# Two graph layers on one core: a new order of small steps at both ends of a graph, and another preparation of the first graph

## The reference, cut to what matters

```python
# layer 0
e0    = leaky(einsum('bid,bjd->bij', x * a0[:, 0], x))      # leaky: v if v >= 0 else 0.2 v
alpha = sigmoid(where(adj == 1, e0, -inf))
x     = layernorm(x + einsum('bij,bjd->bid', alpha, x) + bias)
# layer 1
Hh    = x @ W
s, d  = Hh @ a[:256], Hh @ a[256:]
e     = where(adj != 0, exp(-leaky(s[:, None] + d[None, :])), 0)
x     = layernorm(x + elu((e @ Hh) / rowsum(e)))
```

## Time and profile before

| | before |
|---|---|
| three runs, us | 1290.22, 1290.91, 1291.21 (median 1290.91) |
| profiled execution, us | 1292.38 |
| its span, us | 1290.6 |
| busy, share of the span | PE 94%, weight loads 88%, POOL 81%, DVE 77%, ACT 77% |
| chain that ended last | DVE 34%, POOL 31%, "issue" 22%, PE 6%, ACT 4% |

### The profile page before, as it was taken

How to read it: one execution, slowest core, us unless ns; L and a number is a source line. 1 busy time by engine, 2 the same in 40 slices (tenths; PEclk the granted TensorE clock), 3 DMA queues, 4 the chain that set the end, 5 groups by cost and what they waited for, 6 DMA issues and landing times.

```text
span 1290.6 us, 29789 instructions
## 1 busy us (share of the span) xinstructions
PE 1212.5 (94%) x8898; PEld 1135.5 (88%) x8898; DVE 997.1 (77%) x2499; ACT 988.9 (77%) x2290; POOL 1045.2 (81%) x1052
## 2 busy tenths in 40 slices
PE   5899999999999999999999999999999999999985
PEld 4789899898998989899898988989898898988875
DVE  4678778787877878778787877878778787878855
ACT  4677878778787887878788787887878788787763
POOL 2779797887988889797887988889797887978864
PEclk9999999999999999999999999999999999999988
DMA  9467390854828366381854828366381854818301
GB/s 192 90 118 137 58 178 27 154 106 86 166 40 150 78 131 129 57 164 39 154 106 78 174 37 148 83 129 126 62 162 42 154 106 70 182 34 147 56 9 36
DMA packets 223634, 135.31 MB, mean 105 GB/s; under 512 B 141168, under 2 KB 207088, under 8 KB 223600
## 3 DMA queue, kind: packets, MB, share of 16 engines
q1 hardware_dynamic: 188528, 84.57, 28.0%
q0 software_dynamic: 35072, 50.34, 26.0%
HBM read 101.32 MB, written 16.78 MB: 92 GB/s over the span
## 4 chain that ended last, share of the span: by engine, by line
DVE 34%; POOL 31%; issue 22%; PE 6%; ACT 4%; DVEq 1%; POOLq 1%; DMA 0%; ACTq 0%
POOL coef_lo L394 9%; POOL coef_lo L402 8%; DVE coef L1010 6%; DVE coef L940 5%; POOL rstd L434 3%; DVE stats L1052 3%; DVE reluP L1047 3%; DVE xt_bank L1044 3%; DVE stats L958 2%; DVE coef L931 2%; DVE resid L953 2%; DVE gT_lo L884 2%; POOL var_eps L431 2%; POOL coef_lo L408 2%; POOL h_lo L385 2%
## 5 line engine op out<-in xcount | busy, mean ns | idle before, releaser
L394 POOL TENSOR_TENSOR coef_lo<-coef,coef_hi 128x1024 fp32r<-128x1024 f32 x128 | 307.0, 2405 | 57.4 <-DVE x L970 32.1
L1253 PE MATMUL acc_bank<-h_hi,coef_hi 128*128 128x256 f32 x1024 | 302.5, 295 | 16.6 <-ACT reluP L702 13.9
L402 POOL TENSOR_TENSOR coef_lo<-coef,coef_hi 128x1024 fp32r<-128x1024 f32 (+1 forms) x128 | 294.5, 2308 | 11.5 <-ACT coef_hi L636 11.1
L1253 PE MATMUL acc_bank<-H_hi,coef_hi 128*128 128x258 f32 x1024 | 296.0, 289 | 7.4 <-ACT reluP L702 5.4
L1254 PE MATMUL acc_bank<-H_lo,coef_hi 128*128 128x258 f32 x1024 | 290.6, 284 | 0.0
L1255 PE MATMUL acc_bank<-H_hi,coef_lo 128*128 128x258 f32 x1024 | 290.2, 283 | 0.0
L1255 PE MATMUL acc_bank<-h_hi,coef_lo 128*128 128x256 f32 x1024 | 285.9, 279 | 0.0
L1254 PE MATMUL acc_bank<-h_lo,coef_hi 128*128 128x256 f32 x1024 | 285.8, 279 | 0.0
L1253 PEld LDWEIGHTS acc_bank<-h_hi,coef_hi 128*128 128x128 f32 x1024 | 193.7, 189 | 26.7 <-issue 22.4
L1010 DVE SCALAR_TENSOR_TENSOR coef<-tr_bank,E_col,codeT 128x256 f32<-128x256 f32 (+1 forms) x384 | 193.0, 565 | 24.2 <-POOL coef_lo L402 21.7
L1253 PEld LDWEIGHTS acc_bank<-H_hi,coef_hi 128*128 128x128 f32 x1024 | 194.3, 190 | 11.2 <-issue 8.3
(11 more groups left out here) (91 smaller groups left out, 2814.7 us busy)
## 6 DMA issues: line engine op xcount, KB each, us to landing
code_nat<-in_adj POOLq DMA_DIRECT2D x128, 256.0 KB, 4.8
x_raw<-in_x SPq DMA_DIRECT2D x16, 1024.0 KB, 6.5
xb<-bias_bc SPq DMA_DIRECT2D x16, 1024.0 KB, 8.7
xb<-in_x POOLq DMA_DIRECT2D x16, 1024.0 KB, 12.2
out<-x SPq DMA_DIRECT2D x128, 128.0 KB, 2.0
codeT<-code_nat SPq DMA_TRANSPOSE x128, 3.5
W_ext<-in_L_gnn_W SPq DMA_DIRECT2D x1, 256.0 KB, 3.9
x1T<-in_L_gnn_a SPq DMA_DIRECT2D x1, 256.0 KB, 5.1
```

The source lines that it names most:

```text
L394: nc.gpsimd.tensor_tensor(coef_lo[:, t % 4, :, :], blocks(coef[:, t % 4, :]), f32(coef_hi[:, t % 4, :, :]), ALU.subtract).then_inc(S.lo0, 1)
L402: nc.gpsimd.tensor_tensor(coef_lo[:, t % 4, j0:NT, :], blocks(coef[:, t % 4, j0 * P:N]), f32(coef_hi[:, t % 4, j0:NT, :]), ALU.subtract).t ...
L1253: nc.tensor.matmul(dst, lhs_hi, rhs_hi, start=first, stop=False)
```

## The change

It has two parts. At the borders, in every graph: DVE takes `norm0(7)` ahead of the mask of columns 3 and 4; it takes `residual1(6)` ahead of `mask0_rest(2)`, `row_inverse(7)` between the two, and `residual1(7)` ahead of the whole mask of tile 3; ACT takes `keep_H(6)` and `keep_x1T(7)` ahead of `high1_begin`, the four `high_x` later and spread out, and `high0(b+1, 2)` behind `elu_parts(7)`, `high0(b+1, 3)` behind `tanh_row(b+1, 6)`.

```diff
@@ DVE, graph @@
                     if t == 8:
                         low_H(F, b, 5)
-                        mask1_tiles(b, 0, 4, 3, EDGE)
                         keep_watch(b, prev)
...
+                mask1_tiles(b, 0, 4, 3, EDGE)
                 if nxt:
                     leaky_scores(b + 1, 3)
                 low_H(F, b, 6)
...
                 for t in range(NT):
-                    if t >= 3:
+                    if 3 <= t < 7:
                         row_inverse(F, b, t, prev)
-                    if t >= 4 and nxt:
+                    if 4 <= t < 7 and nxt:
                         mask0_below(b + 1, t - 4, True)
+                    if 4 <= t < 6 and nxt:
                         mask0_rest(b + 1, t - 4)
                     residual1(F, b, t, prev)
                     stats1(F, b, t)
                     moments1(F, b, t)
+                    if t == 6:
+                        row_inverse(F, b, 7, prev)
+                        if nxt:
+                            mask0_rest(b + 1, 2)
+                    if t == 7 and nxt:
+                        mask0_below(b + 1, 3, True)
+                        mask0_rest(b + 1, 3)
@@ ACT, graph @@
                     scale_scores(b + 1, 3)
-                high1_begin(b)
-                if nxt:
-                    high_x(F, b + 1, 0)
                 keep_H(F, b, 6, prev, False)
                 keep_x1T(F, b, 7, prev)
-                if nxt:
-                    high_x(F, b + 1, 1)
+                high1_begin(b)
+                if nxt:
                     scale_scores(b + 1, 4)
...
                 high1(F, b, 1)
                 if nxt:
-                    high_x(F, b + 1, 2)
+                    high_x(F, b + 1, 0)
                     scale_scores(b + 1, 7)
                 high1(F, b, 2)
+                if nxt:
+                    high_x(F, b + 1, 1)
                 high1(F, b, 3)
                 for t in range(NT + 1):
                     if nxt and t == 0:
                         scale_scores(b + 1, 8)
-                        high_x(F, b + 1, 3)
+                        high_x(F, b + 1, 2)
...
                     if t == 1:
                         high1(F, b, 4)
                         if nxt:
+                            high_x(F, b + 1, 3)
                             scale_row(b + 1, 3)
...
-                    if t + 3 >= NT and nxt:
-                        high0(F, b + 1, t + 3 - NT, True)
+                    if nxt and t in (5, 6):
+                        high0(F, b + 1, t - 5, True)
+                    if nxt and t == NT:
+                        high0(F, b + 1, 2, True)
                     if nxt and 3 <= t:
                         tanh_row(b + 1, t - 2)
+                    if nxt and t == NT:
+                        high0(F, b + 1, 3, True)
```

```diff
@@ SP @@
-            load_x(F, 0)
+            for q in range(2):
+                tiles = slice(NT - 2 * q - 2, NT - 2 * q)
+                sp.dma_start(x_raw[:, tiles, :], x_v[0, :, tiles, :]).then_inc(x_part[q], 16)
+            tiles = slice(0, NT // 2)
+            sp.dma_start(x_raw[:, tiles, :], x_v[0, :, tiles, :]).then_inc(F.x_loaded, 16)
...
-            for t in range(NT):
+            for t in range(4):
                 turn_codes(0, t, True)
             sp.wait_ge(weights_loaded, 16 * N_WEIGHT_DMAS)
-            fill_bias()
+            sp.wait_ge(F.xT, 4)
             sp.wait_ge(F.h_lo, 4)
-            sp.wait_ge(F.xT, 4)
+            sp.wait_ge(F.xb_bias, 4)
             load_x(F, 1)
+            for t in range(4, NT):
+                turn_codes(0, t, True)
@@ POOL @@
-            pool.wait_ge(F.x_loaded, 16)
+            pool.wait_ge(x_part[1], 16)
             for t in range(NT):
                 load_adj(F, 0, t, True)
+            for q in range(4):
+                low_x(F, 0, q)
+            pool.wait_ge(weights_loaded, 16 * N_WEIGHT_DMAS)
+            pool.wait_ge(F.x_loaded, 16)
             for c in range(4):
-                low_x(F, 0, c)
-            add_x(0)
+                add_bias_pair(c)
@@ DVE @@
+            high_x_first(0)
+            high_x_first(1)
             dve.wait_ge(cols_loaded, 16 * KINDS)
-            for c in range(4):
-                low_xT(F, 0, c, False)
-            for J in (7, 6, 5, 0):
-                leaky_row(0, J)
-            dve.wait_ge(weights_loaded, 16 * N_WEIGHT_DMAS)
-            extend_weights(1, D)
+            low_xT(F, 0, 0, False)
+            low_xT(F, 0, 1, False)
+            leaky_row(0, 7)
+            low_xT(F, 0, 2, False)
+            leaky_row(0, 6)
+            low_xT(F, 0, 3, False)
+            leaky_row(0, 5)
+            leaky_row(0, 0)
             leaky_row(0, 1)
-            extend_weights(0, D + 1)
-            for t in range(4):
+            keep_W_turned()
+            mask0_below(0, 0, False)
+            mask0_rest(0, 0)
+            leaky_row(0, 2)
+            extend_weights()
+            for t in range(1, 4):
                 mask0_below(0, t, False)
@@ PE @@
+            pe.wait_ge(F.xT_lo, 1)
+            scores(0, 7)
+            pe.wait_ge(F.xT_lo, 2)
+            scores(0, 6)
+            scores(0, 5)
             pe.wait_ge(F.xT_lo, 4)
-            for J in (7, 6, 5, 0, 1):
-                scores(0, J)
-            for t in range(4):
-                mirror(0, t)
-                if t < 3:
-                    scores(0, t + 2)
-            pe.wait_ge(weights_ready, 1)
+            scores(0, 0)
+            scores(0, 1)
+            turn_weights()
+            mirror(0, 0)
+            scores(0, 2)
+            weights_by_a()
+            mirror(0, 1)
+            scores(0, 3)
+            mirror(0, 2)
+            scores(0, 4)
```

More of the change, by code:

```diff
@@ L253, in two_graph_layers @@
         GEN = Signals(sem, "g_", True)
+        x_part = [sem(f"x_part{q}") for q in range(2)]
         cols_loaded = sem("cols_loaded")
@@ L783, in graph @@
                         norm1(F, b, t - 3)
-            act.wait_ge(consts_made, 4)
+            for k, ak in enumerate((a0, a1, a2, a3)):
+                with nc.allow_non_contiguous_dma(reason="one column of 256 values"):
+                    act.dma_start(a_col[:, k, :], ak.rearrange("(c p) o -> p (c o)", p=P)).then_inc(cols_loaded, 16)
+            act.wait_ge(consts_made, 6)
             nc.scalar.activation(scale_col[:, 0:1], zero_col[:, :], ACT.Tanh, scale=0.5).then_inc(table_loaded, 1)
@@ L1395, in graph @@
                     aggregate0(F, b, t, prev)
+                    if t == 0 and not prev:
+                        mirror(b, 3)
+                        pe.wait_ge(weights_ready, 1)
                     if t >= 2:
```

171 lines of the change are left out of this document (100 added, 71 removed).

## The result

| | before | after |
|---|---|---|
| median (runs beside each other), us | 1291.06 (1290.22 to 1291.93, 4 runs) | 1304.67 (1303.03 to 1305.11, 4 runs) |
| profiled execution, its span, us | 1292.38, 1290.6 | 1304.55, 1302.8 |
| mean granted clock of PE | 0.992 | 0.988 |

The ratio is 1.0103, with a 95% interval of 1.0086 to 1.0121: slower by 13.6 us, where 1290.4 was forecast, and 6.7 us outside the range. The order of work at both borders came out as worked out, and the start gave what it was to give. The 13 us are in two things that the sum does not have: a low clock of PE in some graphs of the loop, and a pair of instructions that changed places.

The account below looks back on a forecast made before the run. PE bounds the kernel, and at the border between graphs POOL's chain bounds PE. 11.1 - 1.6 - 10.0 = -0.5 us takes the median from 1290.91 to 1290.4 us, no measurable difference; range 1268 to 1298.

Parts of the forecast that it names:

- The border between graphs: From one graph to the next: `low0(2)` and `transpose_x1(0)` 0.66 us later at 14 borders; 11.1 us slower with the first border.
- the first border: Between the first two graphs: a lucky order of `mask0_rest(2)` and POOL is lost, 1.9 us slower.
- the first rival (1265): Border between graphs: POOL's chain has unseen slack, so 1.0 us per border is kept, 14 times; 1265 us, chance 0.13.
- DVE gets ahead of POOL: Border between graphs: `mask0_rest(4)` runs before `low0(3)`, 0.45 us per border back; 1284, with more luck 1278 us; chance 0.17.
- The border between the layers: Inside each graph: `norm0(7)` 0.8 us earlier, mostly given back waiting for `low_H(6)`; 0.1 us gained per graph, 1.6 us over 16.
- The start: First graph, once: earlier row 0, cheaper W work, `mirror(3)` out of the way, some given back; 10.0 us faster, bounds 6 and 13.
- row 0: Start: ACT's first step earlier and scores running beside the loads of x, row 0 near 15.4; 5.8 us gained.
- the other three: Start: W's products and sums replaced, 3.9 us gained; `mirror(3)` and its tanh moved, 2.7 gained; held-up masks, 2.4 given back.
- the issues of the adjacency loads: Start: POOL's issues beside DVE's two new copies, taken at no cost; by the Trainium skill's rule the sum 1.7 us worse.
- The clock: PE's granted clock: no term in the sum, low clock appearing only in a rival.
- The rival for it: First graph: PE stays at 1.2 GHz through chunks 4 to 11 and two aggregations; 6 us slower, 1296.5 us, chance 0.15.
- The loop away from the borders: Rest of each graph: taken as unchanged, no term; graphs 78.1 us apart instead of 77.6.

Follow-up runs that it names:

- experiment 3: The change with its border between the layers undone; first graph and border between graphs stay changed: 1302.20 us, 1.0087 of before.
- experiment 1: The changed start alone, with both borders as in the kernel before: 1285.55 us, 0.9963 of before.
- experiment 2: The change with its border between graphs undone on DVE and ACT; first graph and border between the layers stay changed: 1285.11 us, 0.9956 of before.
- experiment 4: The full change with 16 identity transposes put on PE ahead of `transpose_x1(0)`: 1296.97 us, 1.0051 of before.
- experiment 9: Changed start with the borders of before, DVE waiting for its own moments ahead of `mask0_rest(7)`: 1281.40 us, 0.9934 of before.
- 11: The kernel before with three more semaphore increments on DVE ahead of the first graph: 1296.56 us, 1.0055 of before.
- 15: The full change with DVE waiting for its own moments ahead of `mask0_rest(7)`: 1294.90 us, 1.0037 of before.
- experiment 6: Changed start, borders of before, `mask0_rest(7)` waiting for POOL's `var_eps`, plus `mask0_rest(2)` ahead of `mask0_below(2)`: 1270.09 us, 0.9841 of before.
- 12: The kernel before with both borders changed and its own first graph: 1305.18 us, 1.0118 of before.

## Why the prediction was wrong

Its own steps first, in their order.

- **The border between graphs, +11.1 us.** Right in mechanism and near in size: experiment 3 against 1 gives 11.9 us without the clock. `low0(2)` was 0.65 us later than before as worked out, and the border 0.72 to 0.8 us longer against 0.66; the first border lost 1.8 us (1.9 forecast). The wait of PE before `transpose_x1(0)` was put at 1.7 us and is 2.0 to 2.1. That the relu's idleness would be no gain in this order was right, and the first rival (1265) with it refuted. One step was near a tie: `mask0_rest(4)` was put 0.5 us behind the start of `low0(3)` and comes 0.06 us behind it. A few hundredths earlier, and the rival "DVE gets ahead of POOL" (0.45 us per border, -6 us) might have come true; no run tries it.
- **The border between the layers, -1.6 us.** Experiment 2 against 1 shows 0.76 us earlier and 0.81 us given back: nothing, at the lower bound of 0 to 0.8 per graph, where 0.1 was taken. The loss of 0.4 us per graph that experiment 2 was to find here stands in experiment 1 without it.
- **The start, -10.0 us.** Right in the sum: 10.8 at the first transpose. The parts offset each other in part: row 0 starts at 16.20 (15.4 forecast), so it gave 5.0 us and not 5.8, and the other three together gave 5.8 and not 4.2; how these split was not measured. `aggregate0(0)` starts at 31.1 (near 32). For the issues of the adjacency loads I took no cost: the eight took 4.50 us together from 6.27, when DVE's two copies (at 4.42 and 5.62, 0.43 us each) were over. They never met, so no run here shows what the Trainium skill's rule (SBUF — State Buffer, "A bandwidth-pool intuition that's wrong") would have cost.
- **The clock, 0 in the sum: the first step that failed.** It is 7.5 us (experiment 4: 7.7). The rival for it looked only at the first graph, where the clock of 0:80 is now 1.00, and at the same time the forecast had PE waiting 1.7 us in each of 15 borders. The earlier trace rows had the low clock behind 2 us of little work. These two were never put side by side, though a bound was to be had from them. In the dip of the first graph before (43.4 to 46.8 us) 16 matmuls of 256 columns start 0.21 us apart instead of 0.12, about 1.5 us lost; one at each of 15 borders is 0 to 22 us. That the rival's price of 6 us is near the measured 7.5 is chance: it was worked out for another place.
- **The loop away from the borders, taken as unchanged: the second step that failed.** The forecast had the distance at 78.1 (77.6 and 0.66, less 0.1); it is 78.75. 0.35 to 0.4 us of that is the turned pair, 4 to 6 us over the run (4.2 in experiment 9, 6.4 in 11, about 5 in 15); most of the rest is 0.14 us more at the border and the 0.1 us that the border between the layers did not give. The rival "DVE gets ahead of POOL" counted such turns as luck to be won, at the border, and priced them at -6 and -12 us. The one that happened was at another place and cost: DVE ahead of POOL is a gain only where POOL's instruction is not the one that is waited for.

A reading in the first paragraph was loose as well: the earlier trace rows leave ACT 15.9 us free and not some 17. No term rests on it.

The sum as measured: -10.8 at the start, +11.9 at the border, 0 between the layers, +7.5 for the clock, +4 to 6 for the pair, 12.6 to 14.6 us against 13.6 measured. So the three terms that were in the forecast give +1 us where it had -0.5. What took the time out of the range is the two terms that were not in it; without the low clock alone it would have been inside (experiment 4: 1296.97).

The stages of the two traces close as well, on the 12.2 us between the profiled runs: -11.0 up to `aggregate0(0)` of graph 1, +12.9 at the 15 borders, +7.5 for the dips, +5.0 for what else the layers of graphs 1 to 14 lost (the pair, and the border between the layers), and -2.2 in the last graph. The last term has no part in the sum above. The kernel before runs 10.2 us of its last graph at half clock, from 1244.8 on, the change, besides its dip, 3.4 us (from 1264.6), and both the last 7 to 8 us; that this makes the 2.2 us was not tested.

## What to carry to other kernels

Where two engines exclude each other, an instruction that just misses the other's start is worth more than its own length: look for the place where it could be ready a few tenths earlier (exchanging two neighbouring instructions gave 15 us in experiment 6), not only for the wait that the engine you care about shows. When a step makes PE idle for 2 us in one place of a loop, count the clock behind it as a cost of that step, with the bound from a dip that the trace already has. And before comparing two versions within half a per cent, look whether an order held by hundredths of a microsecond has turned; a wait that fixes it is cheap.

## What had not been expected of the hardware

- Three semaphore increments on DVE ahead of the first graph, with no work and no reader that waits, made 1290.16 us into 1296.56. The same three on ACT did nothing. With three, a hole of 0.09 us in front of one DVE instruction of the loop was gone, and with sixteen it stood in front of another.
- The granted clock fell to 0.50 behind 1.8 to 2.1 us of idle PE in 6 of 15 borders, in 4 of 15 with the border between the layers undone (experiment 3), and in 2 of 15 with the wait of experiment 9 (15) or with the old start (12), at nearly the same length of the gap. The gap alone doesn't decide it; what else does stays open.
- 16 transposes of 1.91 us together, whose result is overwritten, made the kernel 7.7 us faster.
